# Message layer of a graph network: rows normalised by groups, tail panels sent by SP in two lots, node vector loaded over GpSimd's queue

## The chip, the cores and the metric

The kernel runs on one core of a Trainium2 chip. The metric is the device time of one execution, in microseconds. A run takes all of the program: four layers of a graph network over 3,125 nodes.

## What is computed

The reference applies four layers to the same graph; each ends with a residual sum and a layer norm. The change sits between the second (L1) and the third (L2, the message layer). Cut to that:

```python
x = _layernorm(x + _L1_gnn_ref(x, src, dst, edge_weight1, ...), axis=-1)   # over 64 features
x = _layernorm(x + _L2_gnn_ref(x, node_vec1, edge_index, edge_weight, ...), axis=-1)

def _L2_gnn_ref(mu, x, edge_index, edge_w, W1, W2, W3, W4):
    h_x = relu(x @ W1.T)                  # x is node_vec1, one number a node
    h_e = relu(edge_w[:, None] @ W2.T)
    h_mu = relu(mu @ W3.T)
    dst, src = edge_index[1], edge_index[0]
    cat_feat = jnp.concatenate([h_x[dst], h_e, h_mu[dst]], axis=1)
    agg = jax.ops.segment_sum(cat_feat, src, num_segments=n_nodes)
    agg = relu(agg @ W4.T)
    return relu(h_x + h_mu + agg)

def _layernorm(x, axis=-1, eps=1e-05):
    m = jnp.mean(x, axis=axis, keepdims=True)
    v = jnp.var(x, axis=axis, keepdims=True)
    return (x - m) / jnp.sqrt(v + eps)
```

There are 53,125 edges. All values are float32.

## The kernel before

The 3,125 nodes are 25 blocks (NB) of 125 (B), a block's nodes on 125 partitions. A node table such as t.xa or t.xb is [125, 25, 64]. The sum over a node's neighbours is a product with a matrix of edge counts, t.mat, in bf16: 25 panels of [125, 3128], one for each block of source nodes. Since TensorE multiplies bf16 here, a float32 operand is split into three bf16 parts (split, L778 and on): cast, subtract, cast, subtract. spread (L770) makes one block's sum: 25 matmuls of [125, 192], one a panel.

The program runs in stages, each an nc.Block with a body for each engine; a barrier of all engines stands between blocks. Inside one the engines wait for each other by semaphores only. The order on each engine is the order of the code, written out by hand; there is no planner.

**The edge layer** (edge_network, L976) first has a preparing block, in which q, the nodes' share of the edge network's first layer, is made and split (VectorE L1103 to L1119), while SP loads the weights of the message layer (load_l2_weights, L1443). Then comes the main block, a loop over the 25 destination blocks with five groups of tiles in each (layer1, layer2, by_src, node1, node2). It needs scratch memory, and takes the place of panels 16 to 24 of t.mat for it (HEAD = 16, room, L993). Panels 0 to 15 are loaded by SP in the loop. q lies where panels 16 to 18 belong, and is last read by layer1 of block 24. The main block ends with normalising: VectorE's normalize (L795) with ScalarE's roots (L821).

**The message layer** (message_layer, L1449) is one block of its own:

- ScalarE issues the loads of panels 16 to 24 (L1498 to L1500, two DMAs a panel), then for each of seven groups of four blocks copies the turned rows (keep_columns) and applies relu to the hidden product into feat.
- GpSimd clears x2T and feat, waits for the node vector, which SP loads into two rows of feat (L1483), and clips it in seven pieces: the positive part in one row, the negative part in the other (L1493).
- VectorE makes small weight tables (w1pm, w2pm, mix, we; L1573 to L1583), copies the small products to ge and mix (g_set, L1585 to L1586), and then, for each group, copies base and splits the z product into parts.
- TensorE turns the groups of t.xb (turn, L1520), makes the small products psG, the hidden products psM (hidden, L1534), and the z products psZ from feat and mix (L1558). Then it waits for all tail panels (tail_in) and all parts, and runs spread for 25 blocks.

```python
                pe.wait_ge(tail_in, 32 * (NB - HEAD))
                pe.wait_ge(parts_ready, len(groups))
                for b in range(NB):
                    if b >= 2:
                        pe.wait_ge(kept, b - 1)
                    spread(pe, nc, t.mat, b, parts, psT[b % 2]).then_inc(sums, 1)
```

## Time and profile before

| | us |
|---|---|
| median of 3 runs | 1645.76 (1643.49 to 1646.26) |
| the profiled execution, its time | 1645.85 |
| its span in the profile | 1644.1 |
| TensorE busy | 1414.9 (86% of the span) |
| VectorE busy | 1246.3 (76%) |
| ScalarE busy | 609.4 (37%) |
| GpSimd busy | 44.4 (3%) |

The span runs from the first to the last instruction; 1.75 us lie around it. In the rows below the first number of a timeline row is the time from the span's start, the second how long it was busy, both in us. PE is TensorE, PEld its weight load, DVE VectorE, ACT ScalarE, POOL GpSimd, SP SyncE; a q behind the name is the engine's queue that issues a DMA. A row merges neighbours of the same kind (x18), and its brackets tell how long the engine idled ahead of it and what ended that. The granted clock is a share of 2.4 GHz.

### The profile page before, as it was taken

Reading aid. Unit: us, or ns where it says so; the run is one execution under the profiler, and the core shown is the slowest. Engines: PE = TensorE matmul, PEld = TensorE weight load, DVE = VectorE, ACT = ScalarE, POOL = GpSimd, SP = SyncE. Lnnn points to the kernel's source line nnn. Section 1 sums busy time; section 2 is a strip of 40 time slices with the busy share of each in tenths; the row PEclk is TensorE's granted clock in tenths of the full one; section 3 lists DMA queues with packets and bytes.
Section 4 is the critical chain, followed back from the end, with each engine's and each line's share of the span. In section 5 each row is a group of like instructions: output and inputs, shape, how many; then the busy total and the mean of one; then the engine's idle time right before and its main releaser. Section 6 shows DMA issues by size and latency. Waiting matters only on the chain. (4 is left out here: it accounts for less than half of the span.)

```text
span 1644.1 us, 44005 instructions
## 1 busy us (share of the span) xinstructions
PE 1414.9 (86%) x16795; PEld 1304.8 (79%) x16795; DVE 1246.3 (76%) x3619; ACT 609.4 (37%) x1115; POOL 44.4 (3%) x64
## 2 busy tenths in 40 slices
PE   0745558878996999999999958689999999999997
PEld 0434446668995888888888838689999999999997
DVE  4899988874436888888888856668768777778776
...
GB/s 20 8 1 0 0 47 153 158 138 57 2 1 87 142 138 141 122 156 111 110 73 110 37 111 62 6 1 2 2 2 2 2 2 2 2 2 2 2 3 20
DMA packets 37008, 83.91 MB, mean 51 GB/s; under 512 B 22941, under 2 KB 23957, under 8 KB 36863
## 3 DMA queue, kind: packets, MB, share of 16 engines
...
## 5 line engine op out<-in xcount | busy, mean ns | idle before, releaser
L1751 PE MATMUL L_psA<-L_parts,mat 125*128 125x192 bf16 x6250 | 517.1, 246 | 0.0
L1751 PEld LDWEIGHTS L_psA<-L_parts,mat 125*128 125x128 bf16 x6250 | 515.5, 98 | 1.0 <-DVE L_parts L1828 0.8
L1181 PEld LDWEIGHTS L_ps_pre<-L_drow,mat 128*128 128x128 bf16 x2250 | 129.1, 98 | 30.3 <-issue 1.1
L1690 ACT COPY L_wk<-L_Wk 128x64 f32 (+1 forms) x10 | 2.0, 242 | 391.9 <-PE L_psA L1751 391.9
L1815 DVE TENSOR_REDUCE L_sumr<-L_psA 125x64 f32<-125x192 f32 x225 | 80.5, 358 | 70.9 <-PE L_psA L1751 70.4
L1181 PE MATMUL L_ps_pre<-L_drow,mat 128*128 128x32 bf16 (+3 forms) x2250 | 133.4, 213 | 0.0
L681 PE MATMUL ps_count<-onehot 128*128 128x125 bf16 x1200 | 106.9, 218 | 17.0 <-DVE onehot L644 9.5
L1370 DVE TENSOR_TENSOR L_e<-L_e,mat 128x512 f32<-128x512 f32 x125 | 86.1, 689 | 39.3 <-ACT L_e L1268 39.3
L644 DVE TENSOR_TENSOR onehot<-iota_bf,codes 128x1024 bf16<-128x1024 bf16 x150 | 100.6, 687 | 18.3 <-PE ps_count L681 17.3
L774 PE MATMUL L_psA<-L_gparts,mat 125*128 125x192 bf16 x1250 | 110.3, 250 | 4.5 <-DVE L_gparts L787 4.5
L774 PEld LDWEIGHTS L_psA<-L_gparts,mat 125*128 125x128 bf16 x1250 | 106.8, 101 | 5.2 <-DVE L_gparts L787 4.9
L681 PEld LDWEIGHTS ps_count<-onehot 128*128 128x128 bf16 x1200 | 86.9, 98 | 25.0 <-DVE onehot L644 14.8
L1204 PE MATMUL L_ps_agg<-L_hot,mat 128*128 128x125 bf16 x1500 | 103.5, 219 | 3.8 <-DVE mat L1375 3.8
L1175 PE MATMUL L_ps_pre<-mat,L_pp 125*128 125x512 bf16 x375 | 102.9, 383 | 2.8 <-DVE L_pp L1328 2.8
L1362 DVE TENSOR_TENSOR L_e<-L_ps_z,L_eb 128x512 f32<-128x512 f32 x125 | 85.9, 687 | 23.1 <-PE L_ps_z L1191 21.5
L1204 PEld LDWEIGHTS L_ps_agg<-L_hot,mat 128*128 128x128 bf16 x1500 | 93.8, 98 | 5.6 <-DVE mat L1375 4.1
L420 PE MATMUL ps_slot<-rows,ohr 128*128 128x208 bf16 x450 | 56.8, 294 | 47.0 <-DVE rows L404 32.0
L1267 ACT ACTIVATE mat<-L_e 128x512 bf16<-128x512 f32 x125 | 78.8, 631 | 40.0 <-DVE L_e L1362 37.1
L420 PEld LDWEIGHTS ps_slot<-rows,ohr 128*128 128x128 bf16 x450 | 46.7, 112 | 57.0 <-DVE rows L404 40.8
L1272 ACT CAST mat<-L_e 128x512 bf16<-128x512 f32 x125 | 77.0, 616 | 36.2 <-DVE L_e L1370 36.1
L1375 DVE TENSOR_TENSOR mat<-L_e,mat 128x512 bf16<-128x512 f32 x125 | 85.1, 680 | 0.3 <-ACT mat L1272 0.3
L730 ACT CAST mat<-ps_count 125x1000 f32 (+1 forms) x75 | 78.4, 1045 | 0.1
...
## 6 DMA issues: line engine op xcount, KB each, us to landing
...
mat<-m_d SPq DMA_DIRECT2D x16, 684.2 KB
m_d<-panel SPq DMA_DIRECT2D x13, 684.2 KB
m_d<-xb SPq DMA_DIRECT2D x12, 684.2 KB
mat<-m_d ACTq DMA_DIRECT2D x9, 684.2 KB
...
```

Of the source, the lines that this page charges most:

```text
L420: last = nc.tensor.matmul(ps_slot[k][:, 0:NC * REC], ohr[:, k, j, :], rows[:, k, :, j, :], start=(j == 0), stop=(j == W - 1))
L644: nc.vector.tensor_tensor(to.rearrange("p e (m t) -> p e m t", t=DUP), c.iota1_bf[:].rearrange("p (m t) -> p m t", t=DUP).unsqueeze(1).bro ...
L681: last = nc.tensor.matmul(to, rows, cols[:, 0:B], start=True, stop=more is None)
L774: last = nc.tensor.matmul(ps[:, 0:3 * D], mat[0:B, kb, ob * B:ob * B + P], parts[:, kb].rearrange("p r d -> p (r d)"), start=(kb == 0), st ...
L1175: nc.tensor.matmul(ps_pre[bank][:, 0:hi - lo], pp[k][:, r, :], srow[k][0:B, lo:hi], start=(r == 0), stop=False)
L1181: last = nc.tensor.matmul(ps_pre[bank][:, to:to + n], w, drow[k][:, of:of + n], start=False, stop=(r == 2 and cc == pieces[-1][0]))
L1204: last = nc.tensor.matmul(ps_agg[k][:, 0:B], e2_parts[bank][:, part, i * H:(i + 1) * H], hot[bank][:, i, 0:B], start=(cc == 0 and part == ...
L1362: nc.vector.tensor_tensor(e2[buf(k, g)][:].rearrange("p (i h) -> p i h", h=H), ps_z2[bank][:].rearrange("p (i h) -> p i h", h=H), eb2[:].u ...
L1370: nc.vector.tensor_tensor(e, e, e2_parts[buf(k, g)][:, 0, :], ALU.subtract).then_inc(cut, 1)
L1375: nc.vector.tensor_tensor(part[:, 2, :], e2[buf(k, g)][:], part[:, 1, :], ALU.subtract).then_inc(split_done, 1)
L1751: last = nc.tensor.matmul(ps[:, 0:3 * D], t.mat[0:B, kb, b * B:b * B + P], parts[src][:, kb].rearrange("p r d -> p (r d)"), start=(kb == 0 ...
L1815: v.reduce_sum(r, ps[0:B, 0:3 * D].rearrange("p (r d) -> p d r", r=3), X).then_inc(bank_free, 1)
```

## The change

- The aggregates of the layer norm in front of the message layer are taken at the end of the edge layer: 24 of them ahead of the last node product, the last one behind it. Subtraction, square root, reciprocal and scaling move into the message layer and run group by group (scale_rows), TensorE turning each group when it is scaled (x2_set). The tables bn, mv, std, rstd now lie in t.src1 in both layers (kept_norm_buffers).
- SP issues the tail panels: 16 to 18 at the end of the edge layer's main block, when layer1 of block 24 is done, and 19 to 24 at the start of the message layer. ScalarE issues none.
- GpSimd clears feat first, and loads the node vector over its own queue; ScalarE clips it, in seven pieces, between its copies.
- The right half of mix (a copy of the identity, and the clipped w1) is made in the preparing block of the edge layer. we is made after the scaling. TensorE turns groups 0 and 1 ahead of the small products.

```diff
+def kept_norm_buffers(t):
+
+    old = lambda lo, hi: t.src1[0:B, lo * NB:hi * NB].rearrange("p (b s) -> p b s", s=hi - lo)
+    return old(0, 6), old(6, 8), t.src1[0:B, 8 * NB:9 * NB], t.src1[0:B, 9 * NB:10 * NB]
...
@@ edge_network, preparing block, VectorE @@
                 S(nc.vector.tensor_tensor(t.xb[:], t.xb[:], nb2[:].unsqueeze(1).broadcast_to([B, NB, D]), ALU.add))
+                dve.wait_ge(mix_clear, 1)
+                S(nc.vector.tensor_copy(l2.mix[0:D, D:2 * D], c.ident[0:D, 0:D]))
...
+                dve.wait_ge(l2.w_in, 16 * 7)
+                S(nc.vector.tensor_scalar(l2.mix[D:D + 2, D:2 * D], l2.mix[D:D + 2, D:2 * D], c.sign[D:D + 2, :], 0.0,
+                                          ALU.mult, ALU.max))
...
@@ edge_network, main block, SP @@
                 sp.wait_ge(panels_in, 32 * HEAD)
+
+                sp.wait_ge(pre_done, NG * NB + 1)
+                for i in range(HEAD, HEAD + 3):
+                    for to, of in spans(t.mat[:, i, :], m2_d[i]):
+                        sp.dma_start(to, of).then_inc(l2.tail_in, 16)
...
@@ ScalarE @@
-                roots(nc, act, c, mv, std, var, root)
+                nc.scalar.activation(std[0:1, 0:1], c.eps[0:1, :], ACT.Sqrt)
...
@@ VectorE @@
+                dve.wait_ge(stats, NB - 1)
+                for b in range(NB - 1):
+                    nc.vector.bn_aggr(mv[:, b, :], bn[:, b, :])
                 keep_out(NB - 1, 0)
-                dve.wait_ge(out_kept, NB + 1)
-                dve.wait_ge(stats, NB - 1)
-                S.n = 3 * (NB + 1)
-                normalize(nc, dve, S, t.xa, bn, mv, std, rstd, t.xb, var, root, NB - 1)
+                take_stats(NB - 1)
+                dve.wait_ge(stats, NB)
+                nc.vector.bn_aggr(mv[:, NB - 1, :], bn[:, NB - 1, :])
...
@@ message_layer, SP @@
-                sp.wait_ge(feat_clear, 1)
-                sp.dma_start(feat[D:D + 2, :], a["node_vec1"].partition_broadcast(2)).then_inc(nv_in, 16)
+                for i in range(HEAD + 3, NB):
+                    for to, of in spans(t.mat[:, i, :], m2_d[i]):
+                        sp.dma_start(to, of).then_inc(l2.tail_in, 16)
...
@@ GpSimd @@
+                nc.gpsimd.memset(feat[D:P], 0.0).then_inc(feat_clear, 1)
+                pool.wait_ge(feat_clear, 1)
+                nc.gpsimd.dma_start(feat[D:D + 2, :], a["node_vec1"].partition_broadcast(2)).then_inc(nv_in, 16)
                 for i in range(2):
                     nc.gpsimd.memset(x2T[i][D:P], 0.0).then_inc(zeroed, 1)
-                nc.gpsimd.memset(feat[D:P], 0.0).then_inc(feat_clear, 1)
-                pool.wait_ge(nv_in, 16)
-                for g in range(len(groups)):
-                    nv = feat[D:D + 2, cols(g)]
-                    nc.gpsimd.tensor_scalar(nv, nv, c.sign[D:D + 2, :], 0.0, ALU.mult, ALU.max).then_inc(nv_set, 1)
...
@@ ScalarE @@
-                for b in range(HEAD, NB):
-                    for to, of in spans(t.mat[:, b, :], m2_d[b]):
-                        act.dma_start(to, of).then_inc(tail_in, 16)
+                nc.scalar.activation(std[:], mv[:, :, 1], ACT.Sqrt, bias=c.eps[0:B, :]).then_inc(x2_root, 1)
...
+                def node_values(g):
+
+                    nv = feat[D:D + 2, cols(g)]
+                    nc.scalar.activation(nv, nv, ACT.Relu, scale=c.sign[D:D + 2, :]).then_inc(nv_set, 1)
+
                 keep_columns(0)
+                keep_columns(1)
                 for g, blocks in enumerate(groups):
-                    if g + 1 < len(groups):
+                    if 1 < g + 1 < len(groups):
                         keep_columns(g + 1)
                     act.wait_ge(hmu_ps, g + 1)
                     nc.scalar.activation(feat[0:D, cols(g)], psM[g % 2][0:D, 0:len(blocks) * B], ACT.Relu
                                          ).then_inc(hmut, 1)
+                    if g == 0:
+                        act.wait_ge(nv_in, 16)
+                        node_values(0)
+                    if g + 1 < len(groups):
+                        node_values(g + 1)
...
@@ TensorE @@
                 def turn(g):
+                    pe.wait_ge(x2_set, g + 1)
...
                 turn(0)
-                pe.wait_ge(w_in, 16 * 7)
+                turn(1)
                 pe.wait_ge(w_set, 1)
...
-                turn(1)
                 pe.wait_ge(zeroed, 2)
...
@@ VectorE @@
-                dve.wait_ge(w_in, 16 * 7)
+
+                def scale_rows(g):
+
+                    blocks = slice(groups[g][0], groups[g][-1] + 1)
+                    some = [B, len(groups[g]), D]
+                    S(v.tensor_tensor(t.xa[:, blocks], t.xa[:, blocks], mv[:, blocks, 0:1].broadcast_to(some),
+                                      ALU.subtract))
+                    if g == 0:
+                        dve.wait_ge(x2_root, 1)
+                        S(v.reciprocal(rstd[:], std[:]))
+                    S.wait()
+                    v.tensor_tensor(t.xb[:, blocks], t.xa[:, blocks], rstd[:, blocks].unsqueeze(2).broadcast_to(some),
+                                    ALU.mult).then_inc(x2_set, 1)
+
+                scale_rows(0)
+                scale_rows(1)
                 S(v.memset(w1pm[:, 0:D], 0.0))
...
                 v.tensor_scalar(w2pm[:, 1, :], w2pm[:, 1, :], 0.0, None, ALU.max).then_inc(w_set, 1)
+                for g in range(2, len(groups)):
+                    scale_rows(g)
+                S(v.reduce_sum(we[:], t.wsum[:, :, 0:6].rearrange("p b (s r) -> p b s r", r=3), X))
                 dve.wait_ge(g_ps, 1)
```

How the order on an engine moves is best seen in its rows. VectorE at the end of the edge layer's main block and the start of the message layer, before (src in the later rows is t.src1; UNCONDITIONAL_BRANCH is the step from one block to the next, with the barrier):

```order
L1375 TENSOR_TENSOR mat<-L_e_0,mat 128x512 [waits L1_mid_done]
L1337 TENSOR_TENSOR xa<-L_ps_n,xb 125x64 [waits L1_out_ready]
L803 BN_STATS L_bn<-xa 125x6 [waits L1_net_step,L1_stats_taken,L1_out_kept]
L806 BN_AGGR L_mean_var<-L_bn 125x2 [waits L1_net_step]
L806 BN_AGGR L_mean_var<-L_bn 125x2 x24
L809 TENSOR_TENSOR xa<-xa,L_mean_var 125x1600 [waits L1_var_ready]
L811 RECIPROCAL L_rstd<-L_std 125x25 [waits L1_std_ready]
L814 TENSOR_TENSOR xb<-xa,L_rstd 125x1600 [waits L1_net_step]
L1136 UNCONDITIONAL_BRANCH
L1568 UNCONDITIONAL_BRANCH [waits barrier_Pool_Activation_PE_DVE_SP_release]
L1573 MEMSET L_w1pm 64x64 [waits L2_weights_in]
```

And now (line numbers are those of the changed kernel):

```order
L1391 TENSOR_TENSOR mat<-L_e_0,mat 128x512 [waits L1_mid_done]
L1441 BN_AGGR src<-src 125x2 [waits L1_stats_taken]
L1441 BN_AGGR src<-src 125x2 x23
L1353 TENSOR_TENSOR xa<-L_ps_n,xb 125x64 [waits L1_out_ready]
L1349 BN_STATS src<-xa 125x6 [waits L1_out_kept]
L1445 BN_AGGR src<-src 125x2 [waits L1_stats_taken]
L1147 UNCONDITIONAL_BRANCH
L1594 UNCONDITIONAL_BRANCH [waits barrier_Pool_Activation_PE_DVE_SP_release]
L1603 TENSOR_TENSOR xa<-xa,src 125x256
L1607 RECIPROCAL src<-src 125x25 [waits L2_x2_root]
L1609 TENSOR_TENSOR xb<-xa,src 125x256 [waits L2_msg_step]
L1603 TENSOR_TENSOR xa<-xa,src 125x256
```

The aggregates have moved ahead of the last node product (xa<-L_ps_n,xb), and the two operations over 1,600 columns have left the block: their pieces of 256 columns begin the next one.

TensorE at the start of the message layer, before:

```order
L1524 MATMUL L_psT<-ident,xb 64x125 x4
L1529 MATMUL L_psG<-L_W4a,L_w1pm 66x64 [waits L2_w_parts,L2_weights_in]
L1531 MATMUL L_psG<-L_W4b,L_w2pm 125x64 x2
L1524 MATMUL L_psT<-ident,xb 64x125 x4
L1540 MATMUL L_psM<-L_x2T,L_W3T 64x500 [waits L2_x2T_ready,L2_zeroed]
L1524 MATMUL L_psT<-ident,xb 64x125 [waits L2_x2T_ready,L2_g_set]
```

And now:

```order
L1551 MATMUL L_psT<-ident,xb 64x125 [waits L2_x2_set]
L1551 MATMUL L_psT<-ident,xb 64x125 x3
L1556 MATMUL L_psG<-L_W4a,L_w1pm 66x64 [waits L2_w_parts]
L1558 MATMUL L_psG<-L_W4b,L_w2pm 125x64 x2
L1567 MATMUL L_psM<-L_x2T,L_W3T 64x500 [waits L2_x2T_ready,L2_zeroed]
L1551 MATMUL L_psT<-ident,xb 64x125 [waits L2_x2T_ready,L2_x2_set,L2_g_set]
```

Group 1 is now turned ahead of the small products (psG), and every turning waits for its group to be scaled.

## Rows read from the trace of the kernel before

**Rows 1.** Timeline of VectorE and ScalarE, end of the edge layer

```profile
959.43 1.28 ACT L823 ACT_TABLE_LOAD   x1
...
960.19 0.23 DVE L1337 TENSOR_TENSOR xa<-L_ps_n,xb 125x64 f32<-125x64 f32 x1 [4.24 <-PE L_ps_n L1219]
960.45 0.23 DVE L803 BATCH_NORM_STATS2 L_bn<-xa 125x6 f32<-125x64 f32 x1
960.71 1.76 DVE L806 BATCH_NORM_AGGREGATE L_mean_var<-L_bn 125x2 f32<-125x6 f32 x25
...
962.50 0.32 ACT L823 ACTIVATE L_std<-L_mean_var,eps 125x25 f32<-125x25 f32 x1 [1.78 <-DVE L_mean_var L806]
964.24 0.31 DVE L811 RECIPROCAL L_rstd<-L_std 125x25 f32<-125x25 f32 x1
964.58 1.82 DVE L814 TENSOR_TENSOR xb<-xa,L_rstd 125x1600 f32<-125x1600 f32 x1
```

**Rows 2.** Timeline of all engines, the message layer up to the last part

```profile
966.68 8.88 ACTq L1500 DMA_DIRECT2D mat<-m_d  x18
...
966.72 1.01 PE L1524 MATMUL L_psT<-ident,xb 125*64 125x125 f32 x4 [6.56 <-PEq L1136]
...
967.70 2.78 POOL L1489 MEMSET L_feat<- 64x3125 f32 x1
967.87 2.67 DVE L1579 TENSOR_SCALAR L_mix<-L_mix,sign 2x64 f32<-2x64 f32 x1
970.51 0.26 SPq L1483 DMA_DIRECT2D L_feat<-in_node_vec  x1
...
975.61 1.04 ACT L1506 COPY L_x2T<-L_psT 64x500 f32<-64x500 f32 x2 [12.79 <-issue]
...
976.32 1.90 PE L1540 MATMUL L_psM<-L_x2T,L_W3T 128*64 128x500 f32 x2 [2.78 <-ACT L_x2T L1506]
977.95 12.97 POOL L1493 TENSOR_SCALAR L_feat<-L_feat,sign 2x500 f32<-2x500 f32 x7 [7.46 <-DMA L_feat<-in_node_vec]
...
980.98 1.91 PE L1558 MATMUL L_psZ<-L_mix,L_feat 128*125 128x128 f32 x8
...
984.24 1.14 PE L1558 MATMUL L_psZ<-L_mix,L_feat 128*125 128x128 f32 x8
...
984.93 0.42 DVE L787 TENSOR_TENSOR L_parts<-src,L_parts 125x256 bf16<-125x256 f32 x1
...
986.71 1.14 PE L1558 MATMUL L_psZ<-L_mix,L_feat 128*125 128x128 f32 x8
...
997.23 0.22 DVE L787 TENSOR_TENSOR L_parts<-src,L_parts 125x64 bf16<-125x64 f32 x1
```

**Rows 3.** DMA view, 955 to 1045 us: issues, size of each

```profile
mat<-m_d ACTq DMA_DIRECT2D x9, 684.2 KB
```

**Rows 4.** Windows: length, busy time by engine, granted clock, DMA share, GB/s

```profile
956.00:958.00 2.00, 1.64 (x13) 1.39 (x14) 0.00 (x0) 0.27 (x1) 0.00 (x0) 0.50 0.00 0
...
996.00:998.00 2.00, 0.00 (x0) 0.00 (x0) 1.33 (x6) 0.00 (x0) 0.00 (x0) 0.56 0.51 135
...
975.60:999.10 23.50, 18.09 (x81) 9.93 (x81) 12.63 (x35) 7.33 (x14) 12.43 (x7) 0.79 0.91 212
```

**Rows 5.** Timeline, the first sum of the big product

```profile
999.11 31.12 PE L774 MATMUL L_psT<-L_parts,mat 125*128 125x192 bf16 x352 [4.04 <-DMA mat<-m_d]
1003.36 0.36 DVE L1601 TENSOR_REDUCE L_sumr<-L_psT 125x64 f32<-125x192 f32 x1 [5.91 <-PE L_psT L774]
```

**Rows 6.** Timeline of VectorE, end of the edge layer's preparing block

```profile
525.11 0.88 DVE L1118 TENSOR_TENSOR mat<-mat 125x512 bf16<-125x512 f32 x2
```

**Rows 7.** First 60 us, GpSimd's own DMAs: issue, and DMA view with landing

```profile
20.29 0.74 POOL L110 DMA_DIRECT2D ew<-in_edges  x1 [15.25 <-issue]
...
ew<-in_edges POOLq DMA_DIRECT2D x7, 18.0 KB, 2.0
```

**Rows 8.** Timeline of TensorE, its last first-layer products

```profile
946.97 0.96 PE L1181 MATMUL L_ps_pre<-L_drow,mat 128*128 128x96 bf16 x15
```

26 lines of the change are left out of this document (10 added, 16 removed).

## The prediction

> **What bounds the kernel now.** I read the busy time by stage first, then the timeline of the place where the edge layer hands over to the message layer, then the waits there, then the DMA view. The program is a chain of stages, each closed by a barrier of all engines, so what counts is the time from one barrier to the next; a stage's end is set by its slowest engine. The place is small: from the last rows of the edge layer to the first big product of the message layer the kernel spends about 39 us of 1,644, and TensorE is mostly idle or at its low clock there.
>
> At the end of the edge layer [rows 1] VectorE idles 4.24 us until the last node product at 960.19, and only then does everything that normalising needs: statistics, 25 aggregates (1.76 us), one subtraction over all 25 blocks, a reciprocal (0.31), one product over all blocks (1.82, and the subtraction, of the same shape, as long). It ends at 966.40 and the next stage's first instructions start at 966.68 [rows 2]: a barrier costs 0.28 us.
>
> In the message layer [rows 2] two strands run side by side. Strand one is computing: ScalarE first issues the 18 DMAs of the nine tail panels, 8.88 us, so that its first copy of turned columns starts only at 975.61. The hidden product follows at 976.32, the first z product at 980.98, the next two at 984.24 and 986.71, and the last part is split off at 997.23 + 0.22 = 997.45. Strand two is the tail itself: nine panels, each in a piece of 684.2 KB [rows 3] and a small one of 13 partitions, move at 212 GB/s with the DMA engines 91% busy [rows 4], and TensorE's big product starts at 999.11, after 4.04 us of idling that a DMA ended [rows 5]. So the tail ends last, but only by 1.7 us: whoever takes time from one strand alone gains 1.7 us. The change takes time from both.
>
> **The change, part by part.**
>
> *A. The end of the edge layer.* The 24 aggregates known by then move ahead of the last node product. They cost about 1.7 us and lie in the 4.24 us of idle time [rows 1], so they are free; if that idle time were gone they would cost 1.7. Behind the product there remain the sum (0.23), one statistic (0.23) and one aggregate. 25 aggregates take 1.76, the first of a burst some 0.17, so VectorE is done at 960.19 + 0.23 + 0.23 + 0.17 plus two hand-overs of 0.03, which is 960.9. ScalarE's table load ends at 959.43 + 1.28 = 960.71 [rows 1] and is followed by a one-element square root, about 0.2 us: also 960.9. With the barrier, 0.28, the message layer starts at 961.2 instead of 966.68: **-5.5 us**.
>
> *B. Moved into the preparation of the edge layer:* one 64x64 copy and one 2x64 tensor_scalar on VectorE. There VectorE is the engine that ends last: its last two subtractions end at 525.99 [rows 6]. The copy stands ahead of this splitting, the tensor_scalar behind it. The trace has neither without company; the nearest small VectorE operation is the statistic, 0.23 us [rows 1], and it is 0 if all of it overlaps its neighbours. SP issues the weights that the second waits for early in this stage, so I take that wait as over. Together 0 to 0.5; I take **+0.3 us**, nearer to the row.
>
> *C. The message layer up to the big product.* Times from its first instruction. VectorE now scales the rows by groups. A group is 256 columns; the trace has that shape as a tensor_tensor of 0.42 us [rows 2], and the next independent one can start after some 0.3. Group 0: subtraction to 0.5; meanwhile ScalarE's square root, 0.32 [rows 1]; reciprocal 0.31 to 0.75; product to 1.2. Group 1 ends at 1.95. TensorE turns group 0 from 1.2, 1.01 us at the low clock [rows 2], and group 1 to 3.3; ScalarE copies both by 3.9, since it has no DMAs to issue.
>
> Next VectorE makes the small weights. GpSimd clears feat meanwhile, 2.78 us, and in the trace a tensor_scalar of VectorE beside that same clearing took 2.67 us and ended 0.06 behind it [rows 2]. In the changed order feat is the first thing cleared, so the small weights come through at 2.85 and are all set near 3.5. TensorE makes its three small products (1.3 us, by 4.9), then the first hidden product, 1.90 at the low clock [rows 2], by 6.8. VectorE scales groups 2 to 6, 4 x 0.75 + 0.45, reduces we (0.31) and copies the small products (0.29 + 0.22): the flag g_set is up at 7.7. Behind it TensorE turns group 2 (1.0) and makes the second hidden product (1.9): the first z product can start at **10.6**. Before it started at 980.98 - 966.68 = 14.3.
>
> *The node vector.* ScalarE can clip its first piece only when it has landed. Before, SP issued it at 970.51 and it was there at 977.95, 7.44 us later [rows 2]; the tail filled the DMA engines then. Quiet, a DMA of GpSimd's queue of about that size (18 KB against 25) took 2.0 us [rows 7]. GpSimd issues it at 2.9. Bounds for its landing are 2.9 + 2.0 = 4.9, which hides, and 2.9 + 7.44 + 0.5 = 10.8, the 0.5 because GpSimd's own issue took 0.74 us [rows 7] against SP's 0.26. The tail flows as before, so I take 10.8. A ScalarE pass over 500 columns takes 0.57 (by the copies at 975.61, two in 1.04), so the first z product starts at **11.5**. The other six clippings, 0.57 each, add to a copy and a clipping of the same size, 1.7 us of ScalarE in a round of 2.47 (984.24 to 986.71); they hide behind TensorE. GpSimd's seven, some 1.9 us each, are gone.
>
> The rest runs as before: 997.45 - 980.98 = 16.5 us from the first z product to the last part. That makes 28.0, and 28.1 to the start of the big product. Before it was 999.11 - 966.68 = 32.4: **-4.3 us**.
>
> *The tail.* Three panels are issued by SP once the last first-layer product of block 24 is done; in the trace its last matmuls run at 946.97 + 0.96 = 947.9 [rows 8]. Nine panels took from 966.7 to 999.1, so one takes 3.4 us when they follow each other, plus about 2 at the head. Three are in by 948 + 2 + 10.2 = 960.2, before the barrier. The six left need 2 + 6 x 3.4 = 22.4 us from the stage's start, 5.7 less than the 28.1. So the tail no longer ends last; if it did, each panel would cost 3.4 us.
>
> *Sum.* -5.5 + 0.3 - 4.3 = -9.5 us against the profiled execution's 1645.85 gives **1636.3 us**. That execution stands 0.09 us above the median of the three runs, which I neglect. What follows the big product's start is untouched.
>
> **A rule weighed.** The row says that VectorE's tensor_scalar waited until GpSimd's clearing ended, while ScalarE and TensorE did not. The Trainium skill (SBUF — State Buffer, Who interferes with whom) says the same of copies, casts and tensor_scalars, and it adds the other direction, which speaks against this change: a DMA issued from GpSimd's queue has its descriptors written by GpSimd, and a VectorE operation that holds the shared port keeps it from writing them. No run here shows that second part. By it the node vector's DMA would wait for the small weights that stand queued behind the clearing. Those last from 2.85 to 3.5 by my sum, so this delays the landing by at most 0.7 us, and the start of the big product with it.
>
> **The rivals.** *1. The node vector is served behind the whole tail* (ends on the other side). Place: ScalarE's wait before the first clipping, with TensorE's z products queued behind it. For it: 7.44 us of landing under load against 2.0 quiet. Against: in that case eight or nine of the 18 tail DMAs had been issued before it, and it did not wait for them. If it landed with the last panel, at 22.4, the first z product would start at 23.1, and TensorE, idle from about 10, would do its rounds at the low clock, where a round takes some 5 us against 2.47 for the first 6 us: +3. Then 23.1 + 16.5 + 3 = 42.6, 14.5 later than forecast: 1650.8 us, slower. It decides in this direction from a landing at about 20. Chance 0.04.
>
> *2. The early panels don't run early,* or SP sends the six slowly: all nine then end 32.4 after the start, so the big product starts 4.3 later: 1640.6 us. For it: instruction loads and these transfers share the DMA engines. Against: the DMA engines are at 0.00 while the edge layer ends [rows 4]. Chance 0.08.
>
> *3. The reciprocal, too, waits for the clearing of feat.* Then all of VectorE's chain from there comes 2 us later. g_set is up at 9.7 and the first z product at 12.6: +1.1 us, or +2 if the node vector is early: 1638.0 us. The trace has no reciprocal beside GpSimd. Chance 0.12.
>
> *4. The clock comes off better.* TensorE is granted its low level, 1.2 GHz, at 956 [rows 4]. It gets 2.4 GHz after some 6 us of dense work: eight matmuls of the z product took 1.91 us at 980.98 and 1.14 at 984.24 [rows 2]. It loses it again between 996 and 998, after the z products [rows 4]. So the first of the 25 sums takes 4.1 us instead of about 2 (25 matmuls at the granted 2.4 GHz take half) (999.11 to 1003.3 [rows 5]). If the shorter pause (about 2.5 us instead of 4.0) keeps the clock, or it rises one round sooner, 1 to 3 us more are gained: 1634.3 us. Chance 0.18.
>
> **How the numbers follow.** The forecast has 0.53, the rivals 0.42, and 0.05 is for something not named. Its own range is 1635 to 1638 (B between 0 and 0.5; the node vector between both bounds, up to -0.9; the rule above, up to +0.7; 0.5 for hand-overs). With rivals 2, 3 and 4 the range is **1632.5 to 1641.5**; rival 1 and the unnamed are left out. A measurement of this kernel tells about 0.2%, 3.3 us, from no change. Faster by more than that is everything but rival 1 and most of the unnamed: 0.92. Within: 0.04. Slower: 0.04.
>
> **What would show it.** In the profile after: 24 aggregates between 956 and 958; the first instruction of the message layer at 961 to 962; the tail's waits gone from in front of the big product, and VectorE's last part in their place; that product starting near 989.6; g_set near 7.7 us into the stage; no tensor_scalar on GpSimd. If the big product still waits for a DMA, the tail was mis-sized; if ScalarE waits over 8 us for the node vector, the queue was. If the gain is found behind 1056 on the old scale, it is the clock and not this argument.

## The result and the profile after

| us | before | changed |
|---|---|---|
| median of 7 runs | 1645.57 (1643.39 to 1648.84) | 1640.52 (1637.88 to 1642.78) |
| ratio of changed to before, over the runs | | 0.9973, 95% interval 0.9964 to 0.9983 |
| profiled execution: span | 1644.1 | 1636.4 |
| profiled execution: outside the span | 1.75 | 4.12 |

The kernel is faster: by 5.05 us by the medians and by 4.4 by the ratio, about half of the 9.5 forecast. 1640.5 lies inside the range of the whole forecast and outside the likeliest case's own (1635 to 1638). Over the seven runs of the changed kernel the time outside the span is 4.0 to 4.9 us, with a median of 4.6; the profiled one is near the low end.

Where the two profiled executions differ, stage by stage (each number is the time between two rows of the timelines, us):

| from ... to | before | after | difference | forecast |
|---|---|---|---|---|
| start ... first count product | 227.66 | 225.06 | -2.60 | 0 |
| ... first layer starts | 142.46 | 142.40 | -0.06 | 0 |
| ... edge layer's preparing block starts | 139.30 | 139.57 | +0.27 | 0 |
| ... its main block starts on VectorE | 17.07 | 17.44 | +0.37 | +0.3 |
| ... last node product added | 433.70 | 433.64 | -0.06 | 0 |
| ... message layer starts | 6.49 | 0.99 | -5.50 | -5.5 |
| ... first z product | 14.31 | 12.24 | -2.07 | -2.8 |
| ... last part split | 16.47 | 18.38 | +1.91 | 0 |
| ... big product starts | 1.66 | 0.15 | -1.51 | -1.5 |
| ... first sum reduced | 4.25 | 3.55 | -0.70 | 0 |
| ... fourth layer's first big product | 91.70 | 92.53 | +0.83 | 0 |
| ... last VectorE instruction | 541.29 | 542.73 | +1.44 | 0 |
| ... end | 7.71 | 7.76 | +0.05 | 0 |
| outside the span | 1.75 | 4.12 | +2.37 | 0 |

The first row is not put down to the change: no instruction differs there, and in the profiles below it moves between 225.1 and 227.9 in kernels of either kind. It matters for the account, since the rows behind it add up to no more than -2.7 us. The first layer's row (+0.27) and the fourth layer's (+0.83) also come and go between kernels that do the same work.

The page of the changed kernel: ScalarE has 1123 busy instructions, GpSimd 58.

```profile
span 1636.4 us, 44020 instructions
...
PE 1415.2 (86%) x16795; PEld 1305.0 (80%) x16795; DVE 1244.3 (76%) x3631; ACT 614.2 (38%) x1123; POOL 32.4 (2%) x58
```

The timeline of VectorE at the hand-over, which answers to [rows 1], and on to the copy of the small products:

```profile
953.87 1.60 DVE L1441 BATCH_NORM_AGGREGATE src<-src 125x2 f32<-125x6 f32 x23
958.11 0.22 DVE L1353 TENSOR_TENSOR xa<-L_ps_n,xb 125x64 f32<-125x64 f32 x1 [2.64 <-PE L_ps_n L1235]
958.37 0.23 DVE L1349 BATCH_NORM_STATS2 src<-xa 125x6 f32<-125x64 f32 x1
958.63 0.18 DVE L1445 BATCH_NORM_AGGREGATE src<-src 125x2 f32<-125x6 f32 x1
959.14 0.43 DVE L1603 TENSOR_TENSOR xa<-xa,src 125x256 f32<-125x256 f32 x1 [0.33 <-PEq L1147]
959.49 0.31 DVE L1607 RECIPROCAL src<-src 125x25 f32<-125x25 f32 x1
...
960.62 0.43 DVE L1609 TENSOR_TENSOR xb<-xa,src 125x256 f32<-125x256 f32 x1
...
965.91 0.28 DVE L1625 COPY L_ge<-L_psG 125x128 f32<-125x128 f32 x1
```

The aggregates lie in the idle time, which is now 2.64, and one statistic and one aggregate stand between the product and the next stage. Part A is as forecast to the tenth.

The timeline of all engines in the message layer, with rows for [rows 2] and [rows 5]:

```profile
959.10 2.70 POOL L1504 MEMSET L_feat<- 64x3125 f32 x1 [448.73 <-POOLq L1147]
...
959.10 5.83 SPq L1500 DMA_DIRECT2D mat<-m_d  x12
...
962.10 0.53 POOL L1506 DMA_DIRECT2D L_feat<-in_node_vec  x1 [0.29 <-POOL L_feat L1504]
...
966.48 1.04 PE L1551 MATMUL L_psT<-ident,xb 125*64 125x125 f32 x4 [0.89 <-DVE L_mix L1626]
967.45 1.93 PE L1567 MATMUL L_psM<-L_x2T,L_W3T 128*64 128x500 f32 x2
970.58 1.30 ACT L1527 ACTIVATE L_feat<-L_feat,sign 2x500 f32<-2x500 f32 x2 [4.38 <-DMA L_feat<-in_node_vec]
971.34 2.07 PE L1584 MATMUL L_psZ<-L_mix,L_feat 128*125 128x128 f32 x8 [1.96 <-ACT L_feat L1527]
973.21 1.04 PE L1551 MATMUL L_psT<-ident,xb 125*64 125x125 f32 x4
974.18 1.93 PE L1567 MATMUL L_psM<-L_x2T,L_W3T 128*64 128x500 f32 x2
976.03 1.60 PE L1584 MATMUL L_psZ<-L_mix,L_feat 128*125 128x128 f32 x8
...
978.98 1.14 PE L1584 MATMUL L_psZ<-L_mix,L_feat 128*125 128x128 f32 x8
...
989.87 10.31 PE L774 MATMUL L_psT<-L_parts,mat 125*128 125x192 bf16 x103 [2.53 <-DVE L_parts L787]
```

ScalarE waits 4.38 us for the node vector, and TensorE 1.96 for ScalarE. The big product waits for VectorE's last part and no longer for a DMA. The rounds of the z product, by the starts of the first three, take 4.69 and 2.95 us; before they took 3.26 and 2.47 [rows 2]. The sum of the two differences is 1.91, which is the whole of the row "last part split". The windows say why (length, busy time by engine, granted clock, DMA share, GB/s):

```profile
970.00:972.00 2.00, 0.66 (x3) 0.66 (x4) 0.00 (x0) 1.39 (x3) 0.00 (x0) 0.50 1.03 231
972.00:974.00 2.00, 2.00 (x11) 1.70 (x10) 0.55 (x2) 1.67 (x3) 0.00 (x0) 0.50 1.04 225
974.00:976.00 2.00, 2.00 (x4) 0.29 (x2) 1.35 (x4) 0.57 (x1) 0.00 (x0) 0.50 1.00 241
976.00:978.00 2.00, 2.00 (x14) 1.77 (x13) 0.33 (x1) 1.29 (x2) 0.00 (x0) 0.75 1.03 238
978.00:980.00 2.00, 2.00 (x12) 1.21 (x12) 1.57 (x5) 1.46 (x3) 0.00 (x0) 1.00 0.79 215
```

TensorE had idled for the node vector, and the first window in which it is granted more than 0.50 is the one from 976 to 978: two rounds had begun at 1.2 GHz before it came to 2.4.

### The profile page after: what moved, and what is told of

The parts are those of the page before. It is cut to its first block and busy times, and to the rows that moved or that the text cites. A ratio compares the mean times of both kernels' runs of the same rounds, so it can differ in the third digit from the quotient of the medians.

```text
span 1636.4 us, 44020 instructions
## 1 busy us (share of the span) xinstructions
PE 1415.2 (86%) x16795; PEld 1305.0 (80%) x16795; DVE 1244.3 (76%) x3631; ACT 614.2 (38%) x1123; POOL 32.4 (2%) x58
## 5 line engine op out<-in xcount | busy, mean ns | idle before, releaser
L1197 PEld LDWEIGHTS L_ps_pre<-L_drow,mat 128*128 128x128 bf16 x2250 | 129.0, 98 | 30.3 <-issue 1.1
```

Of the source, the lines that this page charges most:

```text
L1197: last = nc.tensor.matmul(ps_pre[bank][:, to:to + n], w, drow[k][:, of:of + n], start=False, stop=(r == 2 and cc == pieces[-1][0]))
```

## The experiments

Four questions were open: what delays the node vector, what the early panels give, where the 1.4 us in the fourth layer come from, and where the 2.4 us outside the span come from. Three theories stood at the start. Theory 1: the fourth layer's loop runs later because VectorE's program is longer, by eleven records in the trace, so that its code lies elsewhere. Theory 2: the node vector is late because the tail's packets are ahead of it or beside it, not because of its queue. Theory 3: the time outside the span comes with the engine that sends the tail.

| kernel | us | ratio to before, 95% | big product starts, us into the stage | outside the span |
|---|---|---|---|---|
| before_pad13 | 1645.18 | 0.9997 (0.9987 to 1.0008) | 32.8 | 2.0 |
| before_sp_tail | 1645.09 | 1.001 (1.000 to 1.002) | 32.2 | 2.0 |
| before_act_seven | 1644.66 | 0.9991 (0.998 to 1.0002) | 32.8 | 2.2 |
| norm_only | 1641.03 | 0.9976 (0.9965 to 0.9988) | 31.4 | 2.0 |
| norm_back | 1644.59 | 1.0002 (0.9991 to 1.0014) | 29.9 | 4.4 |
| after_pad12 | 1640.43 | 0.9969 (0.9958 to 0.9981) | 30.4 | 4.6 |
| tail_late | 1644.79 | 1.0004 (0.9993 to 1.0015) | 33.0 | 4.5 |
| nv_held | 1638.83 | 0.9962 (0.9949 to 0.9975) | 28.4 | 4.3 |
| nv_act | 1641.93 | 0.9985 (0.9975 to 0.9994) | 30.5 | 4.9 |
| nv_first | 1636.36 | 0.9949 (0.9937 to 0.9961) | 27.5 | 4.5 |
| nv_first_pad12 | 1637.36 | 0.9957 (0.9944 to 0.9971) | 28.3 | 4.4 |
| clip_pool | 1638.78 | 0.9963 (0.995 to 0.9976) | 31.4 | 2.1 |
| mix_back | 1640.13 | 0.9973 (0.996 to 0.9985) | 28.6 | 4.4 |
| pool_seven | 1642.41 | 0.9984 (0.9974 to 0.9994) | 30.8 | 4.1 |
| pool_late | 1642.26 | 0.9985 (0.9975 to 0.9996) | 30.3 | 4.4 |
| clip_pool_act_7 | 1641.39 | 0.998 (0.9971 to 0.9989) | 30.9 | 4.5 |
| nv_first_clip_pool | 1635.90 | 0.9946 (0.9929 to 0.9963) | 26.6 | 2.0 |
| nv_first_act_12 | 1636.25 | 0.995 (0.9936 to 0.9965) | 26.4 | 2.0 |

The third column is read in the one profiled execution, the last is the median over the runs of the kernel. The kernel before, run beside them in six lots, has medians of 1643.99 to 1645.58 and 1.9 to 2.2 outside the span.

### What delays the node vector

**nv_first.** SP issues the node vector ahead of the tail:

```diff
@@ message_layer, SP @@
+                sp.wait_ge(feat_clear, 1)
+                sp.dma_start(feat[D:D + 2, :], a["node_vec1"].partition_broadcast(2)).then_inc(nv_in, 16)
                 for i in range(HEAD + 3, NB):
@@ GpSimd @@
-                pool.wait_ge(feat_clear, 1)
-                nc.gpsimd.dma_start(feat[D:D + 2, :], a["node_vec1"].partition_broadcast(2)).then_inc(nv_in, 16)
```

> The changed kernel, but SP loads the node vector, as soon as feat is cleared, and only then sends panels 19 to 24. Theory 2 (the load of the tail makes the node vector late): it lands about 2 us after its issue at 2.8, by 5; the first z product starts 10.4 to 10.8 us into the stage instead of 12.24, and 16.5 to 17.5 us lie from it to the last part. The tail ends near 25.5, so the big product starts at 27.2 to 28.2 instead of 30.8: 2.5 to 3.5 us below the changed kernel. Rival (the tail now ends last): big product at 29 or later, behind a DMA.

**nv_held.** As the changed kernel, but SP waits with the six panels until the node vector is there:

```diff
@@ message_layer, SP @@
+                sp.wait_ge(nv_in, 16)
                 for i in range(HEAD + 3, NB):
```

> The changed kernel, the node vector still over GpSimd's queue, but SP holds panels 19 to 24 back until it has landed. Theory 2 (load): it lands 2.0 to 2.5 us after its issue at 3.0, so by 5.5, and the panels start 2.5 us later than in the variant where SP sends it; the tail ends near 5.5 + 22.4 = 27.9 and is about level with the parts: big product at 27.5 to 29. Rival (GpSimd's queue is slow by itself): landing 8 us after issue although nothing else moves, the panels start at 11, and the big product only near 33.5, 2.5 us later than in the changed kernel.

**nv_act.** ScalarE issues the node vector behind its first copy, while the tail flows:

```diff
@@ message_layer, GpSimd @@
-                pool.wait_ge(feat_clear, 1)
-                nc.gpsimd.dma_start(feat[D:D + 2, :], a["node_vec1"].partition_broadcast(2)).then_inc(nv_in, 16)
@@ ScalarE @@
                 keep_columns(0)
+                act.wait_ge(feat_clear, 1)
+                act.dma_start(feat[D:D + 2, :], a["node_vec1"].partition_broadcast(2)).then_inc(nv_in, 16)
                 keep_columns(1)
```

> The changed kernel, but ScalarE's queue loads the node vector, behind its first copy, under the same load of the tail. Theory 2 (load, not the queue): it lands 7 to 8 us after its issue at 2.9, the first z product starts at 11.0 to 11.8 instead of 12.24, and about 0.5 to 1 us is gained. Rival (GpSimd's queue is the cause of the 8.5 us): landing 2 to 3 us after issue, first z product at 10.3, and 2 to 3 us gained. Time outside the span 3.9 to 4.9.

The DMA view of the changed kernel and of nv_held, last column us from issue to landing:

```profile
L_feat<-in_node_vec POOLq DMA_DIRECT2D x1, 24.4 KB, 8.5
```

```profile
L_feat<-in_node_vec POOLq DMA_DIRECT2D x1, 24.4 KB, 2.8
```

The same transfer on the same queue takes 2.8 us with the tail held and 8.5 beside it. On ScalarE's queue, beside the tail, it took 8.3 (962.97 to 971.28), and before, on SP's, 7.4 [rows 2]. So it is the load and not the queue: Theory 2 stands. nv_act's first z product came at 11.8 us, as expected, but the clock rose late there too (a first round of 4.69 us), so that the big product is only 0.3 us earlier than in the changed kernel, and its total shows no gain over it (0.9985 against 0.9973). In nv_first the vector is issued at 960.11 and hides behind the hidden product:

```profile
964.03 0.58 ACT L1535 ACTIVATE L_feat<-L_psM 64x500 f32<-64x500 f32 x1 [2.97 <-PE L_psM L1567]
964.64 1.30 ACT L1527 ACTIVATE L_feat<-L_feat,sign 2x500 f32<-2x500 f32 x2
```

The clipping follows with no wait for a DMA, and the first z product starts 10.2 us into the stage instead of 12.2. The big product starts 3.3 us earlier than in the changed kernel, and the total is lower by about 4. nv_held gains the same 2.0 at the z product, but its tail now ends last again (2.1 us of waiting), so it gains less.

### What the early panels give

**tail_late.** No panel is sent in the edge layer, all nine at the start of the message layer:

```diff
@@ edge_network, main block, SP @@
-                sp.wait_ge(pre_done, NG * NB + 1)
-                for i in range(HEAD, HEAD + 3):
-                    for to, of in spans(t.mat[:, i, :], m2_d[i]):
-                        sp.dma_start(to, of).then_inc(l2.tail_in, 16)
@@ message_layer, SP @@
-                for i in range(HEAD + 3, NB):
+                for i in range(HEAD, NB):
```

> The changed kernel, but SP sends all nine tail panels at the start of the message layer, none at the end of the edge layer. The nine take 32.4 us as before, so the big product starts at 32.4 to 32.6 us into the stage, behind a DMA, instead of 30.8 behind the last part: 1.7 us more than the changed kernel, and the three early panels were worth that, not more. Rival: they were worth nothing (big product still near 30.8). Time outside the span: 3.9 to 4.9 as in the changed kernel, by every theory.

TensorE's timeline before the big product:

```profile
989.52 0.48 PE L1579 MATMUL L_psZ<-L_mix,L_feat 128*125 128x128 f32 x2 [0.67 <-DVE L_parts L787]
994.80 5.46 PE L774 MATMUL L_psT<-L_parts,mat 125*128 125x192 bf16 x33 [4.80 <-DMA mat<-m_d]
```

The DMA ends last again and the big product starts at 33.0 instead of 30.8. So the strand of the tail was read rightly, and the early panels are worth 2.3 us here. With the node vector in time they would be worth some 5.5, an estimate from 33.0 and nv_first's 27.5; no run has that pair. The totals differ by more than the 2.3 (1.0004 against 0.9973, about 5 us), and the rest is not assigned.

### The fourth layer's 1.4 us

**after_pad12** and **before_pad13** put small memsets into VectorE's program before the fourth layer, 12 and 13 of them:

```diff
                 v.tensor_scalar(safe[:], deg, 1.0, None, ALU.max).then_inc(deg_set, 1)
+                for i in range(12):
+                    S(v.memset(rstd[0:1, i:i + 1], 0.0))
```

> The kernel before, with 13 one-element memsets added on VectorE at the start of the last layer, where it idles 2.9 us. The change put 13 more instructions ahead of that layer's loop on VectorE. Theory 1 (code placement): the four late reductions of the changed kernel (0.35 us each, at block 24 of each first term) come from where the loop's code lies, so they appear here too: from the first big product of the last layer to the last instruction 542.7 us instead of 541.3, and the time is 1.4 us above before. Rival: they come from the change itself (its tables or semaphores); then the stretch stays at 541.3 and the time is that of before, within 0.3 us.

> The changed kernel, with 12 one-element memsets added on VectorE at the start of the last layer. Theory 1 (code placement): the pause moves about one block ahead, from block 24's reduction to block 23, where VectorE has 0.28 us to spare in each block; the stretch from the last layer's first big product to the last instruction falls from 542.7 to about 541.4, and the time is 1.3 us below the changed kernel. Rival (the change itself delays them): 542.7, and no gain.

In the changed kernel VectorE's timeline has, at block 24 of a term's sum:

```profile
1135.74 0.36 DVE L1855 TENSOR_REDUCE L_sumr<-L_psA 125x64 f32<-125x192 f32 x1 [0.29 <-PE L_psA L1791]
...
1138.15 0.36 DVE L1855 TENSOR_REDUCE L_sumr<-L_psA 125x64 f32<-125x192 f32 x1 [0.63 <-PE L_psA L1791]
...
1140.37 0.36 DVE L1855 TENSOR_REDUCE L_sumr<-L_psA 125x64 f32<-125x192 f32 x1 [0.30 <-PE L_psA L1791]
```

and after_pad12 at the same block:

```profile
1138.06 0.36 DVE L1857 TENSOR_REDUCE L_sumr<-L_psA 125x64 f32<-125x192 f32 x1 [0.30 <-PE L_psA L1791]
...
1140.12 0.36 DVE L1857 TENSOR_REDUCE L_sumr<-L_psA 125x64 f32<-125x192 f32 x1 [0.28 <-PE L_psA L1791]
```

The usual distance is 2.06 us; the changed kernel has one of 2.41 in each of four terms (1135.74 to 1138.15), and 4 x 0.35 is 1.4. It goes with the padding: from big product to last instruction it is 542.73 in the changed kernel and 541.24 in after_pad12. Over all kernels it goes with the length of VectorE's program: the trace holds 6228 records of its queue in before and in norm_back, 6241 in before_pad13, 6251 in after_pad12, all at 541.2 to 541.3; and 6239 in the changed kernel and its twelve other variants, norm_only among them, which stand at 542.6 to 542.9 without exception (nv_first_pad12, with 6251, at 541.25). before_pad13, with two records more than the changed kernel, does not show the delay: there the long distance, 2.41 or 2.42 us, stands behind the 33rd sum of a term instead of the 24th, and the next two, 1.82 and 1.96, make it up, so it costs nothing. So Theory 1 holds in this much: the delay goes and comes with the number of instructions ahead. My reading that 13 instructions by themselves would bring it fell, and what makes the pause no run shows. In the totals 1.4 us cannot be told: after_pad12 has 1640.43 against the changed kernel's 1640.52, on different chips.

**nv_first_pad12** has both edits.

> The changed kernel with the node vector sent by SP ahead of the tail, and with 12 one-element memsets on VectorE at the start of the last layer. Theory 1 (code placement): from the last layer's first big product to the last instruction 541.3 us instead of 542.65, the message layer as in the variant without the memsets (big product 27.3 to 28 us into the stage), so the time is about 1.3 us below that variant's 1636.4. If the late reductions stay, placement isn't their cause.

It ends at 541.25 too, but its total is no better than nv_first's: the intervals overlap.

### Who costs the 2.4 us outside the span

**before_sp_tail** swaps two senders in the kernel before: SP issues the tail, ScalarE the node vector.

```diff
@@ message_layer, SP @@
-                sp.wait_ge(feat_clear, 1)
-                sp.dma_start(feat[D:D + 2, :], a["node_vec1"].partition_broadcast(2)).then_inc(nv_in, 16)
+                for b in range(HEAD, NB):
+                    for to, of in spans(t.mat[:, b, :], m2_d[b]):
+                        sp.dma_start(to, of).then_inc(tail_in, 16)
@@ ScalarE @@
-                for b in range(HEAD, NB):
-                    for to, of in spans(t.mat[:, b, :], m2_d[b]):
-                        act.dma_start(to, of).then_inc(tail_in, 16)
+                act.wait_ge(feat_clear, 1)
+                act.dma_start(feat[D:D + 2, :], a["node_vec1"].partition_broadcast(2)).then_inc(nv_in, 16)
```

> The kernel before with two senders exchanged in the message layer: SP sends all nine tail panels from its start, ScalarE the node vector, as soon as feat is cleared. Nothing else is changed. Inside the span: ScalarE is free from about 4 us on, the first z product comes 1 to 3 us earlier, the parts are done near 29.7 to 30.5 instead of 30.8, but the tail still takes 32.4, so the big product stays at 32.4 to 32.8 and the span that of before within 0.5 us. Outside the span the kernel before spends 1.8 to 2.3 us and the changed one 3.9 to 4.9 in every run. Theory 3: that goes with the sender of the tail (18 transfers of ScalarE's queue now on SP's); then it is 3.9 to 4.9 here, and the time is 2.4 us above before. Rival: it is something else in the change; then 1.8 to 2.3 and the time of before.

2.0 outside: Theory 3 falls. Inside the span the expectation failed. The first z product started 0.7 us earlier, at 13.6, but behind a pause, and the last part was split off later than before, not earlier (32.1 us into the stage against 30.8):

```profile
979.58 2.07 PE L1558 MATMUL L_psZ<-L_mix,L_feat 128*125 128x128 f32 x8 [3.09 <-POOL L_feat L1494]
```

The windows of this kernel, in which the stage starts at 965.97:

```profile
976.00:978.00 2.00, 0.49 (x2) 0.00 (x0) 0.00 (x0) 0.70 (x2) 0.43 (x1) 1.00 0.98 219
978.00:980.00 2.00, 0.42 (x2) 0.42 (x3) 0.00 (x0) 0.00 (x0) 1.91 (x2) 0.66 1.04 250
980.00:982.00 2.00, 2.00 (x11) 1.90 (x11) 0.31 (x1) 0.00 (x0) 1.91 (x2) 0.50 1.00 238
982.00:984.00 2.00, 2.00 (x5) 0.33 (x3) 1.59 (x5) 0.57 (x1) 1.91 (x2) 0.50 1.03 241
984.00:986.00 2.00, 2.00 (x11) 1.72 (x11) 0.00 (x0) 0.58 (x1) 1.91 (x2) 0.64 1.00 244
```

TensorE had been granted 2.4 GHz (1.00), fell to 1.2 in the pause and got back only after 984. The first round takes 4.69 us, and from the first z product to the last part it is 18.47 us instead of 16.47. This kernel differs from the one before only in two senders.

Next the change was cut in two.

**norm_only** is the changed kernel with everything undone but the normalising (the senders, the clipping on GpSimd and mix stand as before). **norm_back** is its mirror:

```diff
@@ edge_network, VectorE @@
-                dve.wait_ge(stats, NB - 1)
-                for b in range(NB - 1):
-                    nc.vector.bn_aggr(mv[:, b, :], bn[:, b, :])
                 keep_out(NB - 1, 0)
-                take_stats(NB - 1)
-                dve.wait_ge(stats, NB)
-                nc.vector.bn_aggr(mv[:, NB - 1, :], bn[:, NB - 1, :])
+                dve.wait_ge(out_kept, NB + 1)
+                dve.wait_ge(stats, NB - 1)
+                S.n = 3 * (NB + 1)
+                normalize(nc, dve, S, t.xa, bn, mv, std, rstd, t.xb, var, root, NB - 1)
@@ message_layer, VectorE and TensorE @@
-                scale_rows(0)
-                scale_rows(1)
...
-                for g in range(2, len(groups)):
-                    scale_rows(g)
...
-                    pe.wait_ge(x2_set, g + 1)
```

> The kernel before with one part of the change alone: aggregates ahead of the last node product, subtraction, root and scaling group by group in the message layer. Tail panels from ScalarE, node vector from SP, clipping on GpSimd, mix and small weights in the message layer as before. Theory A (a part's gain is what its stage shows): the message layer starts 5.5 us earlier after the last node product (0.99 instead of 6.49) and the big product still waits for the tail, 32.4 + 0.3 us into the stage (the root is ahead of the DMAs on ScalarE), so the span is 5.2 us under before's. For the time outside the span, 2.0 us in every kernel of before's family and 4.4 to 4.9 in every one of the changed family: if it comes with the normalising (bn, mv, std, rstd in the kept table, the semaphores that go with it), this kernel has 4.5 outside and gains only 2.7 in all; if it comes with the other parts, it has 2.0 outside and gains 5.2.

> The changed kernel with the normalising put back whole at the end of the edge layer, everything else as changed (early panels and tail from SP, node vector over GpSimd's queue, clipping on ScalarE, mix made ahead). Expected: from the last node product to the message layer 6.49 us as before; the first z product still held by the node vector at about 12.2 us, the big product at about 30.7; the span 1.7 us under before's. Outside the span: the mirror of norm_only, 2.0 if the normalising carries the 2.5 us (total 1.7 us under before), 4.5 if the other parts do (total about 0.8 us over before). If both kernels have 4.5, or both 2.0, neither part alone is it.

norm_only has 2.0 outside and norm_back 4.4: it comes with the other parts. norm_only, one part of the edit alone, has a ratio as good as the whole change's (0.9976 and 0.9973). Its spans gained 3.3 us by their medians where 5.2 were expected; 1.4 of the difference is the fourth layer's, which it has too; the rest is not assigned. norm_back gains its 2.5 us in front of the big product and gives 2.4 back outside: no change.

**clip_pool** clips on GpSimd again, **mix_back** makes mix in the message layer again:

```diff
@@ clip_pool: message_layer, GpSimd @@
+                pool.wait_ge(nv_in, 16)
+                for g in range(len(groups)):
+                    nv = feat[D:D + 2, cols(g)]
+                    nc.gpsimd.tensor_scalar(nv, nv, c.sign[D:D + 2, :], 0.0, ALU.mult, ALU.max).then_inc(nv_set, 1)
@@ ScalarE @@
-                    if g == 0:
-                        act.wait_ge(nv_in, 16)
-                        node_values(0)
-                    if g + 1 < len(groups):
-                        node_values(g + 1)
```

```diff
@@ mix_back: edge_network, preparing block @@
-                S(nc.vector.tensor_copy(l2.mix[0:D, D:2 * D], c.ident[0:D, 0:D]))
...
@@ message_layer, VectorE @@
+                S(v.tensor_copy(l2.mix[0:D, D:2 * D], c.ident[0:D, 0:D]))
...
```

> The changed kernel with the node vector clipped on GpSimd again, in seven pieces behind its clearing of x2T; its load, the tail and all else as changed. The 2.4 us outside the span have so far come with the parts other than normalising, and neither with who sends the tail, nor with the early panels, nor with the queue that loads the node vector. If they come with ScalarE's eight more activations and GpSimd's seven fewer operations: outside 2.0, else 4.4 to 4.9. In the span: the first z product is held until the node vector has landed (11.5) and GpSimd has clipped one piece (1.85 us): 13.4 instead of 12.2 us into the stage, so the big product starts about 1 us later than in the changed kernel, at 31.8.

> The changed kernel with the right half of mix (copy of the identity, clipped w1) made in the message layer again, behind the wait for the small weights. If the 2.4 us outside the span come with these two operations in the preparing block of the edge layer, and the wait for the weights there: outside 2.0, else 4.4 to 4.9. In the span: the two operations lie behind the scaling of group 1 and delay the small weights by about 0.6 us, hidden behind the node vector's landing, so the first z product stays at 12.2 and the big product at 30.8; the preparing block ends 0.3 us earlier, if my term for it (part B) is right. If both kernels stay at 4.5 outside, what is left is TensorE's order (group 1 turned before the small products) and the length of the programs of SP and ScalarE.

clip_pool has 2.1 outside, mix_back 4.4. Inside the span clip_pool did about as expected (first z product at 13.5, big product at 31.4), and mix_back did not: its big product was expected at 30.8 and starts at 28.6, for a reason given below. That left three sides of one edit.

**pool_seven**, **pool_late**, **before_act_seven**: small operations whose results nobody uses.

```diff
@@ pool_seven: the changed kernel, GpSimd @@
+                for i in range(7):
+                    nc.gpsimd.tensor_scalar(spare[D:D + 2, i:i + 1], c.eps[D:D + 2, :], c.sign[D:D + 2, :], 0.0, ALU.mult,
+                                            ALU.max)
@@ pool_late: the changed kernel, GpSimd @@
+                pool.wait_ge(nv_set, len(groups))
+                nc.gpsimd.memset(spare[D:D + 2, 0:1], 0.0)
@@ before_act_seven: the kernel before, ScalarE, in its loop over the groups @@
+                    nc.scalar.activation(spare[D:D + 2, g:g + 1], c.eps[D:D + 2, :], ACT.Relu, scale=c.sign[D:D + 2, :])
```

> The changed kernel, with seven one-column tensor_scalars more on GpSimd behind its clearing (results unused, some 0.1 us each, off every path); ScalarE clips as changed. Span as the changed kernel's. Outside the span: 2.0 if it hangs on GpSimd's number or kind of instructions; 4.4 if on ScalarE's activations or on how late GpSimd still works.

> The changed kernel, with one memset of one column more on GpSimd, which waits until ScalarE has clipped its last piece (result unused). Span as the changed kernel's. Outside the span: 2.0 if it hangs on how late in the program GpSimd works for the last time (about 985 instead of 963.6 us); 4.4 otherwise.

> The kernel before, with seven one-column activations (Relu with a scale per partition, results unused) more on ScalarE, one behind each relu of the hidden product; GpSimd clips as before. They cost 7 x 0.2 us of ScalarE behind TensorE's rounds, so the span stays. Outside the span: 4.4 if it hangs on ScalarE's activations; 2.0 if on GpSimd's.

4.1, 4.4 and 2.2: none of the three moved it. What sorted all kernels so far was how long ScalarE's program is. The records of ScalarE's queue in the traces: 2304 in before_sp_tail and clip_pool, 2321 in before and before_pad13, 2322 in norm_only, 2328 in before_act_seven, all with 2.0 to 2.2 outside; 2310 in norm_back, 2311 or 2312 in the changed kernel and all its other variants, all with 4.1 to 4.9. Two kernels test this in both directions, with seven or twelve activations at the end of ScalarE's part of the message layer:

```diff
@@ ScalarE, ahead of roots @@
+                for i in range(12):
+                    nc.scalar.activation(spare[D:D + 2, i:i + 1], c.eps[D:D + 2, :], ACT.Relu, scale=c.sign[D:D + 2, :])
```

> nv_first (SP issues the node vector ahead of the tail, ScalarE clips) with twelve one-column activations more on ScalarE at the end of the message layer, where it is idle; results unused. ScalarE's program then has 2323 records in the trace instead of 2311. Theory P (the length of ScalarE's program decides, whatever the instructions do): outside the span 2.0, total about 1634. Theory W (ScalarE's clipping or its wait for the node vector decides): 4.4 outside as in nv_first, total about 1636.4. Span as nv_first's in both.

> clip_pool (GpSimd clips, 2.1 outside the span) with seven such activations more on ScalarE at the same place: 2311 records, the number of the changed kernel. Theory P: outside the span 4.4. Theory W: 2.1 as in clip_pool. Span as clip_pool's in both.

nv_first_act_12 has 2.04 (1.67 to 2.26 in six runs) where nv_first had 4.53; clip_pool_act_7 has 4.48 (3.95 to 4.92 in ten) where clip_pool had 2.11 (1.97 to 2.2 in six). The length decides, and the kind of instruction (a DMA, a clipping, an activation that nobody reads) made no difference. Between 2304 and 2310, and between 2312 and 2321, the step was not looked for; nor do these runs show whether the time lies ahead of the first instruction or behind the last.

**nv_first_clip_pool** joins two repairs, the node vector ahead of the tail and the clipping on GpSimd.

> The changed kernel with two repairs: SP issues the node vector ahead of the tail, and GpSimd clips it. The vector lands by about 5 us into the stage, GpSimd's pieces of 1.85 us follow each other and stay ahead of the rounds of 2.5 us, so the first z product is at 10.2 and the big product at 27.5 us as in nv_first, and outside the span there are 2.1 us as in clip_pool. Total: nv_first's ratio 0.9949 less 2.4 us, about 1634.2 against 1645.0 (ratio 0.9934). If the two repairs do not add, it stays at 0.995.

The big product starts at 26.6, outside are 2.0, and the ratio is 0.9946. That is the fastest version by its median against before, but not to be told from nv_first (0.9949) or nv_first_act_12 (0.995), whose intervals overlap it. The 2.4 us outside are seen run by run, as the time less the span. Whether the total gains them is not settled: clip_pool has 0.9963 and clip_pool_act_7 0.998, a step in that direction, though the intervals overlap a little; but between nv_first and the two versions with 2.0 outside they disappear under the spans, whose medians against before's were -11.8 in nv_first, -9.1 in nv_first_clip_pool and -9.0 in nv_first_act_12.

## Why the prediction was right in form and wrong in size

The plan of the stage held, but the sum did not: 9.5 us were forecast, 5.05 came by the medians. What failed are four terms. Two lie in part C, the landing of the node vector (0.7 us too short) and, above all, "the rest runs as before: 16.5 us" (it was 18.4). Two were put at nothing: "what follows the big product's start is untouched" (+1.4 at VectorE) and the time around the span (+2.4).

**A, the end of the edge layer: right.** -5.50 against -5.5, term by term. norm_only, with this part alone, makes 0.9976, 3.4 us of its median.

**B, the preparing block: right as far as it can be read.** +0.37 in the pair (17.07 to 17.44). norm_only and mix_back, which do not have the two operations there, take 16.53 and 16.54. The block also moves by itself: kernels with the two operations take 16.9 to 17.0 us in four profiles and 17.4 to 17.5 in the others.

**C, the message layer: the form right, the size wrong.** Forecast -4.3, measured -1.68. What was right: group 1 is scaled by 1.95 us into the stage (960.62 + 0.43 - 959.10; forecast 1.95), the copies of the small products run at 7 (965.91; g_set was forecast for 7.7), GpSimd issues at 3.0 (forecast 2.9), the tail no longer ends last. Rival 3, a reciprocal held by GpSimd's clearing, did not come: it took 0.31 at 959.49 beside the clearing. Two sizes were off:

- *The node vector's landing.* The bound I took was 10.8; it was there at 11.48 (970.58 - 959.10): 8.5 us of landing, not 7.9. With 0.70 us for one clipping instead of 0.57 the first z product started at 12.24, not 11.5. That is 0.7 of the missing 2.6. The Trainium skill's rule weighed ahead (SBUF — State Buffer, Who interferes with whom), by which GpSimd's descriptors wait for VectorE, is not needed for it: the same load from ScalarE's queue took 8.3. No run here tests the rule. The small weights that it was weighed for were all but done when GpSimd issued (in the changed kernel the last ended at 3.1 us, and GpSimd's issue ran from 3.0 to 3.5), so it had next to nothing to delay.
- *"The rest runs as before: 16.5 us."* This is the step that failed, 1.9 of 2.6. In the kernel before, TensorE worked without a break from 976.32 into its z products at 980.98, and was at 2.4 GHz by the second round [rows 2]: the window from 982 to 984 has 0.85. I let the first z product wait for the node vector, which put an idle 1.96 us ahead of it, and then carried over a duration that had been measured without such a pause. In the twenty profiles the stretch takes 15.7 to 18.5 us, and nearly all of the difference is its first round, 2.5 us with the clock up and 4.7 without. In before_sp_tail, which has of the whole change only SP as the tail's sender, and a pause of 3.09 us ahead of the z products, the stretch is 18.47 and the clock is seen to fall in that pause. mix_back shows it with a first z product at nearly the same place (11.9): its small weights come 1.7 us later, so the second hidden product ends just when the clipped vector is there, TensorE goes into the z products without a pause, the stretch is 16.55 and the big product starts at 28.6. A pause is not all of it. In the ten profiles with one ahead of the z products (1.5 us or more) the first round takes 3.9 to 4.7 us, in the ten without 2.5 to 4.2; and nv_first and nv_first_act_12, with the same instructions up to there and the first z product at 10.2 us in both, have 3.90 and 2.80. So about a microsecond of this term comes and goes by itself, and the 1.9 is one pair's figure.

**"What follows the big product's start is untouched": wrong by +1.4.** The instructions are, but VectorE's run 0.35 us later at four places, and this goes with the length of the code in front. Rival 4 gave back 0.7: the first sum came after a pause of 2.5 us instead of 4.0 and took 3.55 instead of 4.25. The clock was not kept: it was at 1.00 until the big product had begun at 989.87 and fell in the window from 990 to 992. In nv_first_act_12 and nv_first_clip_pool, with the same pause of 2.5 us, it stayed up, and the first sum took 2.33 and 2.34 us. So the price of 1 to 3 us is right where the clock is kept (1.9), and the changed kernel's profile did not have it.

**The sum was made against a profiled execution's time: wrong by +2.4.** I took what lies around the span as fixed at 1.75. It goes with the length of ScalarE's program, 2.0 or 4.4 us, and the change moved it into the dear interval by taking away 18 DMAs and adding eight activations. The Trainium skill (Runtime: NRT & Kernel Launch, The ~15µs preamble/postamble breakdown) lists the steps around a kernel with one figure each and speaks of variation by engine count and DMA setup; clip_pool_act_7 and clip_pool differ in neither and differ by 2.4 us.

In sum, from the count products on: -5.5 + 0.4 - 1.7 for the three parts, which is -6.8, then -0.7 for the first sum, +1.4 at VectorE, +0.8 and +0.2 unassigned, and +2.4 outside. That makes -2.7. With the -2.6 of the first row, which no edit explains, the two profiled executions differ by 5.3; the medians differ by 5.05, and the interval of the ratio reaches from 2.8 to 5.9. So how much of the 5.05 is the change's and how much a chance of the first stretch stays open, and that 1640.5 lies inside the forecast's range is in part luck. Rivals 1 and 2 did not come (the vector did not wait for the whole tail; the big product did not wait for a DMA). With the node vector ahead of the tail, four kernels are 6.6 to 9.2 us below before by their medians, so most of the forecast's 9.5 was there to be had.
